# Cross attention on one Trainium2 core: ready key stacks loaded in one piece, and the 48 row maxima of a batch in one slot

## The reference, cut to what matters

```python
B, N, H = x.shape              # 32, 100, 128
NH = 16; hd = H // NH          # 8
S = context.shape[1]           # 1444
q_c = _ln(x) @ W_qc + b_qc
kv_c = _ln(context) @ W_kvc + b_kvc      # layers 1 and 3: context as it is
k_c, v_c = jnp.split(kv_c, 2, axis=-1)
c_attn_w = jax.nn.softmax(jnp.einsum('bhqd,bhsd->bhqs', q_c, k_c) * scale, axis=-1)
c_attn_out = jnp.einsum('bhqs,bhsd->bhqd', c_attn_w, v_c)
```

## Time and profile before

| | us |
|---|---|
| median of 3 runs | 8284.53 |
| the profiled execution, its own time | 8326.02 |
| its span | 8324.2 |
| PE matmul busy in the span | 5950.0 (71%) |
| DVE busy | 4418.3 (53%) |
| ACT busy | 3049.7 (37%) |
| POOL busy | 1592.6 (19%) |
| row maxima on DVE, L1215 | 2750.0 in 4608 instructions |

### The profile page before, as it was taken

One profiled execution on the slowest core, in us unless ns is written; L12 is line 12 of the kernel. 1 busy time (PEld: TensorE's weight loads), 2 busy tenths in 40 slices (PEclk: granted clock), 3 DMA queues, 4 the chain that ended last, 5 costly groups with the idle time before them and its releaser, 6 DMA issues. The chain is left out here.

```text
span 8324.2 us, 193086 instructions
## 1 busy us (share of the span) xinstructions
PE 5950.0 (71%) x73102; PEld 3970.2 (48%) x73102; DVE 4418.3 (53%) x7950; ACT 3049.7 (37%) x4356; POOL 1592.6 (19%) x866
## 2 busy tenths in 40 slices
PE   4638677777875747778778876789464777777787
PEld 3415455454543525455555544555342555555554
DVE  5536566555664435555555653323553555655555
ACT  2214444444542214344444442213231344444444
POOL 2043222222312022121112200000212121212210
PEclk6656677767766556777677767769555677777767
DMA  3255555555512255555555501110325646555550
GB/s 74 62 79 79 78 73 81 76 78 79 80 26 48 79 81 82 77 74 82 78 78 82 77 14 43 46 36 0 73 55 84 87 70 87 79 79 79 78 78 14
DMA packets 453049, 563.09 MB, mean 68 GB/s; under 512 B 119994, under 2 KB 402394, under 8 KB 442970
## 3 DMA queue, kind: packets, MB, share of 16 engines
q1 hardware_dynamic: 452186, 551.01, 42.2%
HBM read 379.45 MB, written 169.54 MB: 66 GB/s over the span
## 5 line engine op out<-in xcount | busy, mean ns | idle before, releaser
L1215 DVE TENSOR_REDUCE maxima<-ps 100x1 f32<-100x482 f32 (+1 forms) x4608 | 2750.0, 650 | 2263.4 <-PE ps L1047 2059.9
L1170 ACT ACTIVATE probs<-ps 128x800 f32<-128x800 f32 (+1 forms) x2304 | 1810.2, 834 | 2370.9 <-PE ps L1074 2364.0
L1047 PE MATMUL ps<-kst,qst 48*100 48x482 bf16 (+1 forms) x4608 | 1883.8, 517 | 639.3 <-DVE maxima L1215 504.8
L1092 PE MATMUL ps<-probs,vals 128*9 128x100 f32 x36864 | 1381.7, 305 | 251.7 <-issue 250.6
L1074 PE MATMUL ps<-qst,kst 51*128 51x100 bf16 x18432 | 1456.1, 243 | 124.3 <-issue 119.0
L1092 PEld LDWEIGHTS ps<-probs,vals 128*9 128x9 f32 x36864 | 976.7, 108 | 693.9 <-issue 460.2
L1074 PEld LDWEIGHTS ps<-qst,kst 51*128 51x128 bf16 x18432 | 1100.3, 116 | 308.9 <-issue 212.0
L1268 POOL TENSOR_TENSOR kparts<-kf,zero 128x1444 bf16<-128x1444 f32 x192 | 497.7, 2592 | 3762.0 <-ACT kf L1142 3740.5
L1047 PEld LDWEIGHTS ps<-kst,qst 48*100 48x100 bf16 x4608 | 634.9, 143 | 1130.2 <-DVE maxima L1215 803.8
L1019 PE MATMUL ps<-ident,ctok 128*128 128x128 f32 (+1 forms) x1152 | 224.0, 326 | 332.7 <-issue 122.5
L1024 PE MATMUL ps<-ctxT,perm_wk_L 128*128 128x512 f32 (+1 forms) x576 | 326.0, 680 | 44.5 <-DVE maxima L1215 27.8
(11 more groups left out here) (253 smaller groups left out, 5696.3 us busy)
## 6 DMA issues: line engine op xcount, KB each, us to landing
ctx_k_parts<-kparts SPq DMA_DIRECT2D x192, 541.5 KB
kst<-ctx_k_parts SPq DMA_DIRECT2D x192, 541.5 KB
kst<-ctx_k_parts SPq DMA_DIRECT2D x192, 361.0 KB
ctok<-in_ctx_dram SPq DMA_DIRECT2D x96, 704.0 KB
kst<-ctx_k_parts SPq DMA_DIRECT2D x192, 180.5 KB
c<-in_ctx_dram SPq DMA_DIRECT2D x32, 704.0 KB
o_self_sums<-osb SPq DMA_DIRECT2D x24, 800.0 KB
o_sums<-osb SPq DMA_DIRECT2D x96, 200.0 KB
```

The source lines that it names most:

```text
L1047: nc.tensor.matmul(ps[0:N, at:at + w], g.qst[s][row0:row0 + CROWS, j, :], g.kst[s][row0:row0 + CROWS, j, a:a + w], start=True, stop=True). ...
L1092: ins = nc.tensor.matmul(ps[q:q + VW, o:o + N], vals[s][:, kt, h, :], probs[kt % 2][hf][:, CH * e + N * jj:CH * e + N * jj + N], start=(kt ...
L1170: nc.scalar.activation(probs[kt % 2][hf][0:kts[kt], :].rearrange("p (k n) -> p k n", k=2), src, ACT.Exp).then_inc(exp_done, 1)
L1215: nc.vector.reduce_max(maxima[:, col:col + 1], ps[0:N, at:at + widths[c]], AX.X).then_inc(m_read, 1)
```

## The change

1. DRAM now holds the stacks ready made, `kscr[s]` of 128 rows by 8 x 1444. `sp_keys_out` writes each part as often as the stack has it: 6 DMAs instead of 2 (`K_RUNS`: 3, 2 and 1 slots, for two halves), twice the bytes. `sp_stacks` loads a stack with one DMA of 128 partitions instead of 6 of 24, 16 and 8, so with the rows of ones: 128 rows instead of 96.
2. The queries' repeats are made by a broadcast source: 6 DMAs instead of 12, the same bytes.
3. `MAX_A = 0`: all 48 tiles of batch b+1 are in slot b. `dve_rowmax` and `dve_negmax` stand behind the last tile, `pe_turn_max` behind the last step, and `TURN_KT` is gone.
4. The rows of ones: in layer 0 one memset and 6 DMAs write them into DRAM once; the other memsets of key stacks (DVE and POOL) in this phase are gone.

```diff
-    MAX_A = 16
+    MAX_A = 0
...
-    TURN_KT = 8
+    K_RUNS = ((0, 3), (3, 2), (5, 1))
+    KW = 16 * 2 * len(K_RUNS)
+    Q_SLOTS = ((0, 3), (3, 2), (5, 1))
...
-    ring_of = lambda kt: ([4 * kt, 4 * kt + 1, 4 * kt + 2] + (["turn"] if kt == TURN_KT else [])
-                          + list(PREPS.get(kt, ())) + [4 * kt + 3])
+    ring_of = lambda kt: ([4 * kt, 4 * kt + 1, 4 * kt + 2] + list(PREPS.get(kt, ())) + [4 * kt + 3]
+                          + (["turn"] if kt == KT - 1 else []))
...
+        def slot_rows(s, e, first, n):
+
+            return g.kscr[s].rearrange("(e r d) (j n) -> e (d j) r n", e=2, d=HD, j=PAIRS)[e, :, first:first + n]
...
-                if kt == TURN_KT:
-                    pe_turn_max(slot)
...
+            pe_turn_max(slot)
...
-                if x == 4 * TURN_KT + 1 and k1 is not None:
+                if x == MT - 1 and k1 is not None:
                     dve_negmax(k1)
...
-            rows = [g.kscr[s][e].rearrange("t (d j) n -> (t d) (j n)", j=PAIRS) for e in range(2)]
-            for first, end, src in ((0, 24, 0), (24, 40, 0), (40, 48, 0)):
-                for e in range(2):
-                    sp.dma_start(g.kst[s][HALF * e + first:HALF * e + end, :, :].rearrange("p j n -> p (j n)"),
-                                 rows[e][src:src + end - first, :]).then_inc(k_loaded[s], 16)
-            for slot, part in enumerate(SLOT_Q):
-                for e in range(2):
-                    at = HALF * e + HD * slot
-                    sp.dma_start(g.qst[s][at:at + HD, :, :].rearrange("p j n -> p (j n)"),
-                                 g.qx[bass.ds(b, 1), e, part].rearrange("a (d j) n -> (a d) (j n)", j=PAIRS)).then_inc(qst_loaded[s], 16)
+            sp.dma_start(g.kst[s][:, :, :].rearrange("p j n -> p (j n)"), g.kscr[s]).then_inc(k_loaded[s], 16)
+            for e in range(2):
+                for part, (first, copies) in enumerate(Q_SLOTS):
+                    at = HALF * e + HD * first
+                    sp.dma_start(g.qst[s][at:at + HD * copies, :, :].rearrange("p j n -> p (j n)"),
+                                 g.qx[bass.ds(b, 1), e, part].rearrange("a (d j) n -> a d (j n)", j=PAIRS)
+                                 .to_broadcast([copies, HD, PAIRS * N])).then_inc(qst_loaded[s], 16)
...
-            for e in range(2):
-                sp.dma_start(g.kscr[s][e].rearrange("t r n -> r t n"), parts[HALF * e:HALF * e + HALF, :, :]).then_inc(k_written[s], 16)
+            for first, n in K_RUNS:
+                for e in range(2):
+                    sp.dma_start(slot_rows(s, e, first, n), parts[HALF * e:HALF * e + HALF, 0:n, :]).then_inc(k_written[s], 16)
```

More of the change, by code:

```diff
@@ L1040, in pe_max @@
             if t == 0:
-                wait(g.pe, k_loaded[s], 16 * 6 * (r + 1))
-                wait(g.pe, qst_loaded[s], 16 * 12 * (r + 1))
+                wait(g.pe, k_loaded[s], 16 * (r + 1))
+                wait(g.pe, qst_loaded[s], 16 * 6 * (r + 1))
             pe_ring_free(slot, x)
@@ L1289, in pool_split_keys @@
             p = k.prev()
-            wait(pool, k_written[p.s], 16 * 2 * (p.r + 1))
+            wait(pool, k_written[p.s], KW * (p.r + 1))
             pool_copy(parts[:, 0, :], kf[:, :]).then_inc(split, 1)
@@ L1319, in sp_stacks @@
             wait(sp, st_full, H2 * (b - LAG + 1))
-            wait(sp, k_written[s], 16 * 2 * (r + 1))
-            rows = [g.kscr[s][e].rearrange("t (d j) n -> (t d) (j n)", j=PAIRS) for e in range(2)]
-            for first, end, src in ((0, 24, 0), (24, 40, 0), (40, 48, 0)):
-                for e in range(2):
-                    sp.dma_start(g.kst[s][HALF * e + first:HALF * e + end, :, :].rearrange("p j n -> p (j n)"),
-                                 rows[e][src:src + end - first, :]).then_inc(k_loaded[s], 16)
-            for slot, part in enumerate(SLOT_Q):
-                for e in range(2):
-                    at = HALF * e + HD * slot
-                    sp.dma_start(g.qst[s][at:at + HD, :, :].rearrange("p j n -> p (j n)"),
-                                 g.qx[bass.ds(b, 1), e, part].rearrange("a (d j) n -> (a d) (j n)", j=PAIRS)).then_inc(qst_loaded[s], 16)
+            wait(sp, k_written[s], KW * (r + 1))
+            sp.dma_start(g.kst[s][:, :, :].rearrange("p j n -> p (j n)"), g.kscr[s]).then_inc(k_loaded[s], 16)
[5 more added lines that the diff above has]
+                                 .to_broadcast([copies, HD, PAIRS * N])).then_inc(qst_loaded[s], 16)
         def sp_negmax(k):
@@ L1424, in _ @@
                     dve_ctx_rstd(first)
-                nc.vector.memset(g.kst[0][:, :, :].rearrange("p j n -> p (j n)").bitcast(F32), ONE_PAIR).then_inc(stacks_set, 1)
+                if normed:
+                    nc.vector.memset(g.kst[0][:, :, :].rearrange("p j n -> p (j n)").bitcast(F32), ONE_PAIR).then_inc(stacks_set, 1)
                 for b in range(-3, 1):
@@ L1439, in _ @@
                     pool_norm(first)
-                for s in range(1, LAG):
-                    nc.gpsimd.memset(g.kst[s][:, :, :].rearrange("p j n -> p (j n)").bitcast(F32), ONE_PAIR).then_inc(stacks_set, 1)
                 for b in range(-3, 1):
@@ L1454, in _ @@
                     sp_load_ctx(known(b).k(0))
+                if normed:
+                    sp.wait_ge(stacks_set, 1)
+                    for s in range(LAG):
+                        for e in range(2):
+                            rows = slice(HALF * e + CROWS, HALF * e + HALF)
+                            sp.dma_start(g.kscr[s][rows, :], g.kst[0][rows, :, :].rearrange("p j n -> p (j n)")).then_inc(ones_written, 16)
+                    sp.wait_ge(ones_written, 16 * 2 * LAG)
                 for b in range(-3, 1):
-                    if b == -2:
-                        sp.wait_ge(stacks_set, LAG)
                     sp_slot(known(b))
@@ L1985, in program @@
     g.qx = nc.dram_tensor("cross_q_parts", (B, 2, PARTS, HALF, N), BF16).ap()
-    g.kscr = [nc.dram_tensor(f"ctx_k_parts{s}", (2, PARTS, HALF, S), BF16).ap() for s in range(LAG)]
+    g.kscr = [nc.dram_tensor(f"ctx_k_stack{s}", (P, PAIRS * S), BF16).ap() for s in range(LAG)]
     g.oself = [nc.dram_tensor(f"o_self_sums{s}", (P, 4 * CH), F32).ap() for s in range(LAG)]
```

1 line of the change is left out of this document (added).

## The result

The changed kernel takes **7464.26 us** (median of 4 runs, 7459.73 to 7470.51) beside 8289.32 us for the one before (median of 4, 8252.77 to 8319.61). The ratio is 0.901, 95% interval 0.897 to 0.904: 9.9% faster. The prediction was 7890 (7600 to 8440).

A forecast was written before the change was run, and what follows sets the result against it. PE's waits for transposed maxima and late instructions, with the slow clock behind them, were taken to bound the kernel; 29 slots x 15.2 us gained 441, edges lost 41, so 8326.0 gave 7926, beside the median 7890 us (7600 to 8440).

The forecast's parts named there:

- Missing instructions: PE's stops on "issue" within a slot: 7 us today, scaled by the longest DMA backlog to 2.9 us a slot.
- The first rival: No stops for instructions at all, the backlog being shorter than what PE has in hand: 252 us less, 7640; chance 0.20.
- the chain: Slot's end: last max matmul and reduces, transpose, negation and 6 small DMAs, with nothing to cover them: 8.7 us.
- The slot without stops: A cross attention slot before adding the stops for instructions: 27.35 + 13.7 + 8.7 us.
- the six steps: The slot's last six steps, without preparations, at full clock: 2.29 us each, 13.7 us.
- The first part: The slot's first six steps, with preparations, were to stay at 27.35 us.
- Layer 0: DVE's subtraction at the slot's end waits about 1.9 us for POOL's normalisation (bounds 0 and 2.9); slot 54.6 us.
- The wide load: Loading a stack of 2.96 MB with one DMA of 128 partitions at 346 GB/s: 8.6 us.
- The slow load: Rival: the stack's load takes 28.5 us and SP's list sets the slot, 60 us or more; about 8550 us, chance 0.05.
- SP's queue: SP's list of DMAs in a slot ends at about 36 of 52 us, so nothing waits for SP.
- The clock rival: Steps 6 to 11 run at 1.2 GHz: 6.7 us a slot, 8470 us in full; chance 0.17 for more than four slow.
- The maxima: The wait in step 8 and its three slow steps go; an uncovered 8.7 us at the slot's end replaces them.

The follow-up runs named there:

- e1: Changed kernel with the row maxima spread over two slots again (MAX_A = 16, transpose in step 8); 7430.76 us, ratio 0.890 to the kernel before.
- e10: e6 with the transpose behind the value matmuls, now of step 9, and every preparation about one step earlier; 6844.55 us, ratio 0.824 to the kernel before.
- e4: Changed kernel plus a copy of the whole stack within DRAM, read by nothing, behind each wide load; 7591 us, ratio 0.917 to the kernel before.
- e11: Changed kernel with each stack loaded by 2 DMAs of 64 partitions instead of one of 128; 7875 us, ratio 0.949 to the kernel before.
- e3: Changed kernel with each stack loaded by 8 DMAs of 24, 16, 8 and 16 partitions instead of one of 128; 9393 us, ratio 1.133 to the kernel before.
- e6: e1 with the transpose and negation in step 10 instead of 8 (TURN_KT = 10); 7144.86 us, ratio 0.860 to the kernel before.
- e2: Kernel before with MAX_A = 0 and the transpose at the slot's end, nothing else changed; 8431.20 us, ratio 1.017 to the kernel before.

## Why the prediction was wrong, point by point

- **"Missing instructions", the failed step.** I put 7 us a slot before and 2.9 after, scaled by the longest backlog. Both ends were off. e1, which has this part of the change alone, gains 9.1 us a slot; and in the changed kernel 2.0 us of stops are left in all the slots together (1.1 ahead of L1099, 0.9 ahead of L1081). The 2.9 alone are 252 us. Scaling by the backlog took the wrong quantity: keys out (9.7 us, the backlog I had blamed) stop next to nothing within a slot (4.3 us in all of e10, where they go out at full clock; but a jump of the loop beside them is some 2 us longer), e4's 18 us of wide transfers hardly anything, e11's 15 us of 64 partitions 1.9 a slot. The first rival, no stops and 7640 us, was the right case, and I gave it 0.20 though the earlier trace rows held evidence for it. Its reason, a backlog shorter than what PE has in hand, is not what e4 shows. I also read the 3.77 us of the earlier trace rows as a late block behind the DMA backlog; they lie beside the loop's jump, and in the changed kernel the chain at the slot's end covers it.
- **The slot without stops.** For layers 1 and 3 I had 27.35 + 13.7 + 8.7 = 49.8; it is 48.0 and 47.9. The chain (8.7; measured 8.5) and the six steps (13.7; 14.3) were right. The first part was not "27.35 us stays" but 25.5: the slot of the earlier trace rows has two stops of 0.46 and 0.42 us in that part itself, which lengthen their steps by 0.7 each, and I had taken it for a clean one; the other 0.4 lie in its two slow first steps. Net of the three parts, 1.85 us in 58 slots are 107 us.
- **Layer 0.** The slot is 51.7, my 54.6 less the 2.9 of stops. But the number is luck, since the reason I gave does not hold: L1242 takes 0.37 us there (median of 29), not 1.9 more. DVE is busy 1018.9 us in 29 slots of layer 0 against 868.2 in layer 1, 5.2 us a slot. That this fills it is likely, and was not tried.
- **The sum.** Against the 400 us forecast, 855.5 were measured; the 455 between are 252 (stops after), 109 (the 87 slots otherwise), 27 (the 30th slots, which I had not counted) and 67 (starts and the rest, for which I had put 0 with 10 either way).
- **The wide load** was sized right: 8.6 us against 9.2. The slow load, chance 0.05, is excluded here, and e3 shows that it would have been worse than my 8550.
- **The last slot but one**: 49.5 forecast, 49.7 measured.
- **SP's queue**: 36 us forecast, 36.5 measured from the first small DMA to the last of L1362. For today's list I wrote 44.5 us and worked out 45.0; 45.0 is right, and nothing hangs on it.
- **The clock rival** did not come: in the last six steps the clock is at 1.00. What would have made it come stays open. The clock stayed up through four slots with one wait of 0.8 us each and fell in other slots with the same wait (both e10), and it fell behind two waits of 0.8 and 1.1 us in a part that I would have called dense (e6).
- **The maxima.** I counted the move as a gain of 1.6 us a slot (58.4 - 7 to 49.8). From e1 to the changed kernel it is 0.1, and the last slots take it back. The wait of step 8 was exchanged for a chain that costs about as much, though it also covers the loop's jumps. In e2 the move is a loss: its 87 slots take 5166.0 us, 85 more than before, and the last slots but one 41 more, against 109 us between the two profiled executions (134 between the medians). 72 of the 85 us are in layer 0, where the move costs 36 us beside the wide load too; why it costs there stays open.

## What to carry to other kernels

If an engine stands on "issue" in the middle of a group, look for a transfer of few partitions that is in flight at that time, and widen it to 128 partitions before trying anything about the engine's own order, even if that doubles the bytes. Judge a DMA by GB/s beside its share: 0.98 at 86 GB/s and 0.98 at 408 are different things to everyone else on the engines. And place a reduction's tail (transpose, negation, small DMAs) so that work stands on both sides of it: where one wait of 0.8 us was left of 7.9 us, slots went from 48 to 39 us at best, more than the waits themselves had taken. A hardware loop's jump back can stand behind such a wait; look for it once the wait is gone.

## What the runs showed of the hardware

- Loads into 128, 64 and 8 to 24 partitions moved the same 2.96 MB in 9.2, 15.4 and 34.1 us, at equal DMA share.
- Instructions came on time beside the first (2.0 us of stops in all slots of the changed kernel), not beside the last (1322.6 us in the program of e3, single stops up to 16.1 us outside a phase's start). An instruction block's packet took 0.95, 1.37 and 1.92 us (medians) inside these three loads.
- PE's jump back to the head of a hardware loop took 3.3 to 6.4 us in e10 (21 jumps), and 19 of them showed as a stop of PE, 82.5 us together, with no load of a stack in flight, but with keys going out. With neither beside it, a jump took 3.3 to 4.0 us (105 jumps in five kernels).
- TensorE's clock was at 2.4 GHz through the 156.1 us of e10's window, in which PE's longest wait was 0.8 us, and at 1.2 GHz for 13 us behind two waits of 0.8 and 1.1 us in e6. In e10 it also fell, for 6 us and more, in a slot whose longest wait was 0.8 us.
- DVE's 16x100 subtraction in float32 took 0.25 us alone and 3.0 us (3.005 to 3.011 in all 29 slots of layer 3 of e1) while POOL was at work on two-input operations.
